# A two-layer graph network on one core: the start of each gather group is granted by SyncE instead of paced by memsets on GpSimd

## The chip, the cores and the metric

The kernel runs on one core of one Trainium2 chip. Its time is the device time of one execution in microseconds (us), taken as the median of three runs. Engines are named as in the profile: PE is TensorE (PEld its weight loads), DVE is VectorE, ACT is ScalarE, POOL is GpSimd, SP is SyncE. A small q behind a name (POOLq, SPq) is the engine's sequencer: register operations, waits, semaphore increments and DMA issues that run there and are not counted as busy time. A semaphore is a counter; an engine waits until it has reached a value, and instructions and DMAs add to it when they end.

## The reference

There are 12500 nodes with 64 features and 212500 edges (source, target, 8 edge features, one of 16 types), sorted by target.

```
h = relu(layernorm(x))
x = x + segment_sum over edges of  h[src] @ W_rel[type],  into dst          # layer 1
h = relu(layernorm(x))
msg = relu(concat(h[src], h[dst], attr) @ W1 + b1) @ W2 + b2
x = x + segment_sum(msg, dst)                                              # layer 2
```

## The kernel before

**Tiling.** The edges are worked through in 208 groups of 1024 (8 tiles of 128 edges), the last one shifted back so that it is full. Eight groups are one turn of a loop (`it` counts 26 turns, `u` the 8 groups of a turn). Layer 1 takes all 208 groups, then layer 2 all 208.

**What a group does.** POOL fetches the 1024 source rows by eight indirect DMAs (`gather`, 128 rows of 256 bytes each): in layer 1 from `h_table`, in layer 2 from `p_table`, which holds h @ W1's upper part. The rows land in `rows[:, u]`, one of eight buffers, and count in `rows_in[u]`. In layer 1 PE multiplies each tile of rows with a one-hot of slot and type that DVE makes (`onehot`) and counts `slots_summed` twice per group; ACT copies the sums (`slots`); every second group PE applies the 16 type weights and places the result (`place`), and DVE adds it to the accumulator `acc`. Once per turn a chunk of 480 finished nodes is normalised and multiplied with W1, and SP stores it to `p_table` and `q_table`. In layer 2 PE makes the edge and target parts of the message (`w_attr`, `q_blk`), DVE adds the gathered rows to them (`slots<-ps,rows`, counted by `pre_added`), ACT applies relu, PE and DVE sum and place.

**What sets the order around the change.** Each engine runs its own program in order; semaphores tie them together. POOL's main loops are `turn_of_rows` (layer 1) and `turn_of_groups` (layer 2). Before group g it waits, in this order, for: `spaced`, that is until all memsets behind the gathers of group g-1 are done; `batch_in`, every fourth group, the indices; `slots_summed` (layer 1) or `pre_added` (layer 2), until the engines have finished group g-2. Then it issues eight pairs of one gather and one memset of a single element, `spacer`, which counts `spaced`. The first 16 groups of layer 1 are outside this: their gathers (six groups from `x`, ten from `h_table` with `src_tab` as index) have no memsets and no wait for `spaced`, and from the seventh on wait only for the group that used the buffer before.

SP's loop in layer 1 (`batch`, `store_pq`) loads the next indices, four groups at a time, when `slots_summed` shows the buffer free, and stores the chunk of the turn before. In layer 2 (`pairs`) it waits every second group for `pre_added`, reads two group bases from SBUF (`TENSOR_LOAD base_row`) and issues two loads of `q_win`; every fourth group it adds a load of indices and one of edge features, once per turn the store of a finished chunk.

`wait_apart` is a wait with an increment of a counter that nobody reads; on the sequencer it is one instruction (`EVENT_SEMAPHORE`), with a register operation ahead of it where the value depends on the loop.

Of the kernel before, what the change touches and what calls it, by code (L numbers as in the profile page):

```python
# [6 lines left out]
def gnn_kernel(nc, x, src, dst, edge_attr, edge_type, rel_weight, w1, b1, w2, b2, out):  # L7
# [23 lines left out]
    T = 8  # L31
# [6 lines left out]
    U = 8  # L38
# [30 lines left out]
    EVEN = (HG - 1) // 16 * 16  # L69
    IDS = 16 * 4  # L70
    assert PG * T == AC * CI and U - EG == PG and EG < U and G % U == 0 and G % 2 == 0 and LN0 + LP * LI == N and 0 < DUP and NC % AC == 1 and U == 8

    ctx = ExitStack()
    with ctx:
# [3 lines left out]
        def sem(name):  # L78
            return ctx.enter_context(nc.semaphore(name))
# [176 lines left out]
        rows_in = [sem(f"rows_in_{u}") for u in range(U)]  # L256
        spaced = sem("spaced")

# [279 lines left out]
        def _(sp):  # L538
# [46 lines left out]
            with sp.If(fits > 0):  # L585
                def batch(it, k):

                    g = it * U + k * B
                    wait_apart(sp, slots_summed, 2 * (g + B))
                    sp.dma_start(idx[:, k * B:(k + 1) * B, :], src_tab[:, bass.ds(g, B), :]).then_inc(batch_in[k], 16)  # L590

                sp.wait_ge(prep_copied, 4)
                sp.wait_ge(weights_in, 16 * NWL)
                sp.dma_start(w_attr[T * F:2 * T * F], w_attr[0:T * F]).then_inc(weights_copied, 16)
                with sp.Fori(2, NIT) as it:
                    for k in range(U // B):
                        batch(it, k)
                    store_pq(it - 2, chunk_nodes)

                for k in range(U // B):  # L600
                    sp.wait_ge(slots_summed, 2 * (AHEAD + G - U + (k + 1) * B))
                    sp.dma_start(idx[:, k * B:(k + 1) * B, :], src_tab[:, k * B:(k + 1) * B, :]).then_inc(batch_in[k], 16)
                store_pq(NC - 1, chunk_nodes)
            with sp.Else():
# [13 lines left out]
            with sp.If(fits > 0):  # L618
# [24 lines left out]

                def pairs(it, ahead=2):

                    for u in range(1, U, 2):
                        g = it * U + u
                        if ahead or u < V:
                            wait_apart(sp, pre_added, AHEAD + g + 1)
                            load_q(g + V - 1, (u + V - 1) % V)  # L650
                        if u % B == B - 1 and (ahead or u < B):
                            k = u // B
                            if ahead:
                                load_idx((it + 1) * U + k * B, k)
                            if ahead == 1 and k == U // B - 1:
                                load_last_attr()
                            else:
                                load_attr((it + 1) * U + k * B if ahead else 0, k)
# [5 lines left out]
                pairs(0)  # L664
                with sp.Fori(1, NIT - 2) as it:
                    pairs(it)
                    store_out(it - 1, chunk_nodes)
                pairs(NIT - 2, ahead=1)
                store_out(NIT - 3, chunk_nodes)
                pairs(NIT - 1, ahead=0)  # L670
                store_out(NC - 1, chunk_nodes)
# [8 lines left out]
        def _(pool):  # L680
# [42 lines left out]
            with pool.If(fits > 0):  # L723
# [28 lines left out]
            with pool.If(fits > 0):  # L752
                def turn_of_groups(it, last=False):
                    for u in range(U):
                        wait_apart(pool, spaced, T * ((NIT - 2 + it) * U + u + 1) - SKIP)
                        if u == 0:
# [4 lines left out]
                        for j in range(SKIP if last and u == U - 1 else 0, T):  # L761
                            gather(p_table, u, j, rows_in[u])
                            pool.memset(spacer[:, j:j + 1], 0.0).then_inc(spaced, 1)  # L763

                with pool.Fori(0, NIT - 1) as it:
                    turn_of_groups(it)
# [772 lines left out]
```

## Time and profile before

| | |
|---|---|
| three runs | 4940.25, 4952.87, 4954.87 us; median 4952.87 |
| profiled execution | 4951.48 us, its span 4949.3 us (2.2 us lie outside the span) |
| POOL busy | 3439.7 us, 69% of the span |
| PE busy | 2744.9 us, 55% |
| DVE, ACT busy | 1470.4 us, 582.2 us |
| chain that ended last | POOL 34%, issue 23%, unknown 21%, PE 12%, DVE 6% |
| gathers in the paced loops | 1533 in layer 1, 1661 in layer 2 |

The span is from the first to the last instruction. A row of the timeline gives the start, the duration, engine, line, operation, what is written and read, a count, and in brackets how long the engine sat idle before it and what ended that; "issue" means that the profile shows nothing that it waited for, "remote" that the semaphore's last change has no instruction that the profile could name.

### The profile page before, as it was taken

The page shows a single profiled execution, that of the slowest core. Times are in us where ns is not written, and L with a number is a line of the kernel's source. Part 1 is how long each engine was busy: PE and PEld are TensorE (multiplying, and loading weights), DVE is VectorE, ACT ScalarE, POOL GpSimd, SP SyncE. Part 2 cuts the span into 40 slices and gives each one's busy share as a digit, 9 for nine tenths or more (in the row PEclk, how much of TensorE's full clock was granted, in tenths as well). Part 3 has the DMA queues.
Part 4 walks back from the last instruction along what each step waited for, and adds up shares of the span by engine and source line. Part 5 has one row for each costly group of instructions (what it writes and reads, how often), then busy time and mean ns, then how long its engine had stood idle before and what let it go on. Part 6 is the DMA issues. An engine that isn't in the chain of part 4 may idle for free.

```text
span 4949.3 us, 40507 instructions
## 1 busy us (share of the span) xinstructions
PE 2744.9 (55%) x10310; PEld 1528.5 (31%) x10310; DVE 1470.4 (30%) x2002; ACT 582.2 (12%) x1139; POOL 3439.7 (69%) x6536
## 2 busy tenths in 40 slices
PE   2656555565565655566655454555555554555555
PEld 1434333343343333333422222222222222222222
DVE  6323222222222222222233332333233232332333
ACT  3111111111111111111110000000000000000000
POOL 7567676676776776676756676777777767767676
PEclk8777777777777767776766666666666666666666
DMA  4111111111111111111111111111111111111111
GB/s 100 21 25 25 27 25 24 24 27 24 25 27 25 25 27 25 24 27 24 25 29 29 29 29 30 29 30 31 29 31 31 29 29 30 29 30 32 28 30 26
DMA packets 391188, 144.16 MB, mean 29 GB/s; under 512 B 321650, under 2 KB 337323, under 8 KB 391163
## 3 DMA queue, kind: packets, MB, share of 16 engines
q0 software_dynamic: 106304, 109.07, 11.5%
q1 hardware_dynamic: 282245, 34.18, 4.8%
q10 hardware_dynamic: 2614, 0.62, 0.1%
q8 instruction: 10, 0.16, 0.0%
q14 instruction: 15, 0.12, 0.0%
HBM read 129.03 MB, written 12.83 MB: 29 GB/s over the span
## 4 chain that ended last, share of the span: by engine, by line
POOL 34%; issue 23%; another core or an unknown queue 21%; PE 12%; DVE 6%; DMA 2%; DVEq 1%; ACT 1%; POOLq 0%; ACTq 0%; SPq 0%
POOL rows L710 31%; PE ps L1462 3%; PE ps L1379 2%; PE ps L1461 2%; POOL spacer L743 2%; PE ps L1466 1%; DVE z_slot L1230 1%; DVE slots L1219 1%; DVE q_blk L1243 1%; DMA rows<-p_table,idx 1%; DVEq L1234 1%; POOL spacer L763 1%; PE ps L1386 1%; DMA rows<-h_table,idx 1%
## 5 line engine op out<-in xcount | busy, mean ns | idle before, releaser
L710 POOL DMA_INDIRECT rows<-p_table,idx x1661 | 1580.3, 951 | 728.9 <-issue 510.2
L710 POOL DMA_INDIRECT rows<-h_table,idx x1533 | 1451.9, 947 | 695.9 <-issue 417.5
L1379 PE MATMUL ps<-onehot,rows 128*64 128x256 f32 x3328 | 742.2, 570 | 500.6 <-DMA rows<-h_table,idx 407.2
L1461 PE MATMUL ps<-w_attr,attr_t 64*128 64x512 f32 x416 | 368.0, 980 | 1087.4 <-DVE q_blk L1243 753.8
L1095 DVE TENSOR_TENSOR onehot<-key,ps 128x2048 f32<-128x2048 f32 x209 | 473.9, 2278 | 532.0 <-remote 344.6
L1379 PEld LDWEIGHTS ps<-onehot,rows 128*64 128x64 f32 x3328 | 364.5, 199 | 787.4 <-issue 693.2
L1219 DVE TENSOR_TENSOR slots<-ps,rows 128x512 f32<-128x512 f32 x208 | 143.8, 692 | 1263.0 <-remote 698.4
L1386 PE MATMUL ps<-w_types,slots 128*128 128x128 f32 x3328 | 464.2, 297 | 86.6 <-issue 85.3
L1386 PEld LDWEIGHTS ps<-w_types,slots 128*128 128x128 f32 x3328 | 430.6, 209 | 163.7 <-issue 157.8
L1461 PEld LDWEIGHTS ps<-w_attr,attr_t 64*128 64x128 f32 x416 | 87.8, 262 | 1125.2 <-issue 1124.8
L1462 PE MATMUL ps<-q_blk,onehot 128*128 128x512 f32 x416 | 405.9, 1077 | 0.0
L890 ACT COPY slots<-ps 128x512 f32<-128x512 f32 x416 | 241.0, 588 | 1020.3 <-remote 456.7
L1466 PE MATMUL ps<-relus,onehot 128*128 128x512 f32 x416 | 336.8, 906 | 0.9 <-DVE z_blk L1226 0.9
L1158 DVE TENSOR_TENSOR acc<-acc,ps 64x128 f32 x208 | 58.2, 280 | 889.7 <-PE ps L1393 519.3
L951 ACT ACTIVATE relus<-slots 128x512 f32<-128x512 f32 x208 | 131.1, 630 | 1421.5 <-DVE slots L1219 1083.4
L1226 DVE TENSOR_TENSOR z_blk<-ps,blocks 128x512 f32<-128x512 f32 x208 | 143.2, 689 | 327.8 <-remote 204.5
L1393 PE MATMUL ps<-place,nodes_t 128*64 128x256 f32 x416 | 150.2, 499 | 130.5 <-ACT nodes_t L894 125.8
L1230 DVE TENSOR_REDUCE z_slot<-z_blk 128x64 f32<-128x512 f32 x208 | 209.2, 1006 | 0.0
L1462 PEld LDWEIGHTS ps<-q_blk,onehot 128*128 128x128 f32 x416 | 96.0, 287 | 271.7 <-issue 271.7
L1243 DVE TENSOR_TENSOR q_blk<-ps,blocks 128x512 f32<-128x512 f32 x208 | 141.4, 680 | 98.7 <-remote 78.7
L1456 PEld LDWEIGHTS ps<-q_win,onehot 128*128 128x128 f32 x416 | 109.4, 266 | 191.5 <-issue 191.5
L1470 PEld LDWEIGHTS ps<-onehot,z_slot 128*65 128x65 f32 x416 | 93.2, 224 | 222.0 <-issue 219.5
(142 smaller groups left out, 1939.3 us busy)
## 6 DMA issues: line engine op xcount, KB each, us to landing
rows<-p_table,idx POOLq DMA_INDIRECT x1661
rows<-h_table,idx POOLq DMA_INDIRECT x1533
attr<-in_edge_attr_dram SPq DMA_DIRECT2D x52, 128.0 KB
q_win<-q_table SPq DMA_DIRECT2D x208, 32.0 KB
p_table<-pq_out SPq DMA_DIRECT2D x25, 120.0 KB
q_table<-pq_out SPq DMA_DIRECT2D x25, 120.0 KB
out_dram<-xs SPq DMA_DIRECT2D x25, 120.0 KB
xs<-in_x_dram SPq DMA_DIRECT2D x6, 480.0 KB, 6.3
```

The lines of the kernel that those rows point to most:

```text
L710: pool.indirect_dma_start(rows[:, u, t, :], None, table, bass.IndirectOffsetOnAxis(ap=at, axis=0)).then_inc(s, 16)
L890: act.copy(to, slot_ps[:, u % 2, t, :].rearrange("p t (r w) -> p t r w", w=W0)).then_inc(slots_copied, 1)
L1095: dve.tensor_tensor(onehot[:, b], key0[:, bass.ds(g, 1), :].rearrange("p a (t c) -> p (a t) c", c=1).broadcast_to([P, T, C0]), iota_ps.rea ...
L1219: dve.tensor_tensor(presum[:, u % 2, 0:T * D], pre_ps[:, u % 2, :], rows[:, u].rearrange("p t d -> p (t d)"), ALU.add).then_inc(pre_added, 1)
L1230: dve.tensor_reduce(z_slot[:, u, 0:D], z_blk[:].rearrange("p (t d) -> p d t", d=D), X, ALU.add).then_inc(z_slotted, 1)
L1243: dve.tensor_tensor(by_tile(q_blk[:, u % 2, :]), q_ps.rearrange("p (a d) -> p a d", a=1).broadcast_to([P, T, D]), own_tile, ALU.mult).then ...
L1379: last = pe.matmul(slot_ps[t % 2 * D:(t % 2 + 1) * D, b, t // 2, :], rows[:, u, t, :], onehot[:, b, t, :], start=True, stop=True)
L1386: last = pe.matmul(nodes_ps, slots[:, b, r, :], w_types[:, r, :], start=(r == 0), stop=(r == R - 1))
L1393: last = pe.matmul(win_ps, nodes_t[:, h * D:(h + 1) * D], place[:, h, :], start=(h == 0), stop=(h == 1))
L1461: pe.matmul(pre_ps[:, u % 2, :], attr_t[half, u // 2, :], w_attr[half].rearrange("k j d -> k (j d)"), start=True, stop=False)
L1462: pe.matmul(pre_ps[:, u % 2, :], oh1_t[:, u, :], q_blk[:, u % 2, :], start=False, stop=True).then_inc(pre_made, 1)
L1466: pe.matmul(z_ps, oh1[:, u, :], relu_rows[:, u % 2, :], start=True, stop=True).then_inc(z_made, 1)
```

## The change

The memsets and the semaphore `spaced` go. Two semaphores come: POOL counts `asked`, SP counts `granted`. At the start of each group POOL waits for its grant, counts `asked` for the next group, waits as before for `batch_in` and for `slots_summed` or `pre_added` of group g-2, and issues the eight gathers one behind the other. SP waits for the request, six times in layer 1 and three times in layer 2 with one increment of the unread counter each, and then counts `granted`. SP's loads and stores are put between the grants: in layer 1 the indices behind the second and sixth grant of a turn and the chunk's store behind the fifth; in layer 2 the `q_win` loads, the indices and the edge features behind every second grant, for the group two before, and the store behind the second.

```
...
+    PACE = (6, 3)
...
-        spacer = sb("spacer", [1, T], fp32)
...
+        def asks(it, u, second):
+
+            return (NIT - 2 if second else -2) * U + it * U + u + (0 if second else 1)
...
+                def turn_of_loads(it, last=False):
+                    for u in range(U):
+                        for _ in range(PACE[0]):
+                            wait_apart(sp, asked, asks(it, u, False))
+                        sp.sem_inc(granted, 1)
+                        if u == 1:
+                            batch(it, 1)
+                        if u == 4:
+                            store_pq(it - 2, chunk_nodes)
+                        if u == 5 and not last:
+                            batch(it + 1, 0)
+                        if u == 5 and last:
+                            first_batch(0)
...
+                def turn_of_pairs(it, ahead=2, first=False, store=True):
+                    for u in range(U):
+                        if not first or u >= 1:
+                            for _ in range(PACE[1]):
+                                wait_apart(sp, asked, asks(it, u, True))
+                            sp.sem_inc(granted, 1)
+                        if u % 2 == 1 and (not first or u >= 3):
+                            before, v = back(it, u, 2)
+                            loads_after(before, v, ahead if u >= 3 else min(ahead + 1, 2))
+                        if u == 1 and store:
+                            store_out(it - 2, chunk_nodes)
...
-                pool.sem_inc(spaced, T)
+                pool.sem_inc(asked, 1)
 
                 def turn_of_rows(it, last=False):
                     for u in range(U):
-                        wait_apart(pool, spaced, T * ((it - 2) * U + u + 1))
+                        wait_apart(pool, granted, asks(it, u, False))
+                        if not last or u < U - 1:
+                            pool.sem_inc(asked, 1)
 
                         if u % B == 0:
                             wait_apart(pool, batch_in[u // B], 16 * (it - 1))
                         wait_apart(pool, slots_summed, 2 * AHEAD + 2 * (it * U + u - 1))
                         for t in range(SKIP if last and u == U - 1 else 0, T):
                             gather(h_table, u, t, rows_in[u])
-                            pool.memset(spacer[:, t:t + 1], 0.0).then_inc(spaced, 1)
...
```

The loop of layer 2 on POOL changes in the same way. `loads_after` is the body of the old `pairs`.

Two places show what stands where. First POOL's program at the start of the layer 1 loop, before. `L710` is the gather, `L359` a wait with a register, a wait that carries no own line stands at the next instruction.

```order
46 L745 UNCONDITIONAL_BRANCH
47 L745 ISA
48 L359 ISA [waits spaced]
49 L359 ISA [waits batch_in_0]
50 L710 DMA rows<-h_table,idx 128x64 [waits slots_summed]
51 L743 MEMSET spacer 1x1
52 L710 DMA rows<-h_table,idx 128x64
53 L743 MEMSET spacer 1x1
```

The same place after the change, with the next group; `L364` is the wait, `L740` the gather.

```order
48 L364 ISA [waits granted]
49 L364 ISA [waits batch_in_0]
50 L740 DMA rows<-h_table,idx 128x64 [waits slots_summed]
51 L740 DMA rows<-h_table,idx 128x64 x7
52 L364 REGISTER_ALU
53 L364 ISA [waits granted]
54 L740 DMA rows<-h_table,idx 128x64 [waits slots_summed]
55 L740 DMA rows<-h_table,idx 128x64 x7
```

A group is now eight gathers in a row, and the wait ahead of it is no longer for work of POOL itself but for a count of SP.

Then SP's loop of layer 1, before: `idx<-src_tab` are the index loads, `p_table` and `q_table` the chunk's stores.

```order
37 L590 ISA [waits slots_summed]
38 L590 DMA idx<-src_tab 128x32
39 L359 ISA
40 L590 ISA [waits slots_summed]
41 L590 DMA idx<-src_tab 128x32
42 L581 ISA [waits pq_copied]
43 L581 DMA p_table<-pq_out 120x256
44 L581 DMA q_table<-pq_out 120x256
```

After the change (the repeated waits and the increments set no row of their own and stand at the next one):

```order
38 L364 REGISTER_ALU [waits asked]
39 L364 ISA [waits asked]
40 L595 ISA [waits slots_summed]
41 L595 DMA idx<-src_tab 128x32
42 L364 REGISTER_ALU
43 L364 REGISTER_ALU [waits asked] x2
44 L586 ISA [waits asked,pq_copied]
45 L586 DMA p_table<-pq_out 120x256
46 L586 DMA q_table<-pq_out 120x256
47 L364 REGISTER_ALU
48 L364 ISA [waits asked]
49 L595 ISA [waits slots_summed]
50 L595 DMA idx<-src_tab 128x32
```

The index loads and the store now stand behind grants, and a grant that follows them in the program waits until they are issued.

## Rows read from the trace of the kernel before

**Rows 1.** The page, part 1: busy time of each engine.

```profile
PE 2744.9 (55%) x10310; PEld 1528.5 (31%) x10310; DVE 1470.4 (30%) x2002; ACT 582.2 (12%) x1139; POOL 3439.7 (69%) x6536
```

**Rows 2.** POOL's groups by line: busy, mean ns | idle before, releasers.

```profile
L710 POOL DMA_INDIRECT rows<-p_table,idx x1661 | 1580.3, 951 | 728.9 <-issue 510.2 <-DVE slots L1219 198.9 <-POOL spacer L763 19.8
L710 POOL DMA_INDIRECT rows<-h_table,idx x1533 | 1451.9, 947 | 695.9 <-issue 417.5 <-remote 193.9 <-PE ps L1379 78.8
```

**Rows 3.** The memsets by tile: ns min/median/max, first and last start.

```profile
L763 POOL MEMSET spacer<- x1661: 88/89/91, 2502.8 to 4926.8; 1x1 f32 x185
L743 POOL MEMSET spacer<- x1533: 88/89/91, 218.3 to 2473.9; 1x1 f32 x192
```

**Rows 4.** Timeline of POOL, layer 1, 1498 to 1584 us.

```profile
1501.17 0.95 POOL L710 DMA_INDIRECT rows<-h_table,idx  x1 [3.63 <-remote]
...
1502.42 0.95 POOL L710 DMA_INDIRECT rows<-h_table,idx  x1 [0.21 <-issue]
...
1511.92 0.95 POOL L710 DMA_INDIRECT rows<-h_table,idx  x1 [0.96 <-issue]
...
1514.00 0.95 POOL L710 DMA_INDIRECT rows<-h_table,idx  x1 [1.04 <-issue]
...
1536.19 0.94 POOL L710 DMA_INDIRECT rows<-h_table,idx  x1 [2.84 <-remote]
...
1581.23 0.95 POOL L710 DMA_INDIRECT rows<-h_table,idx  x1 [1.06 <-issue]
```

**Rows 5.** POOL's waits: total us, times, longest.

```profile
POOL rows L710 <- issue: 971.0, 3161, 27.9
POOL rows L710 <- remote: 205.0, 71, 4.5
POOL rows L710 <- DVE slots L1219: 198.9, 48, 8.4
POOL rows L710 <- PE ps L1379: 83.6, 15, 23.8
```

**Rows 6.** Timeline of POOL, the gathers without memsets, 103 to 194 us.

```profile
103.69 0.94 POOL L710 DMA_INDIRECT rows<-h_table,src_tab  x1 [4.83 <-PE ps L1379]
...
132.44 0.94 POOL L710 DMA_INDIRECT rows<-h_table,src_tab  x1 [0.30 <-issue]
137.89 0.95 POOL L710 DMA_INDIRECT rows<-h_table,src_tab  x1 [4.50 <-remote]
...
160.87 0.94 POOL L710 DMA_INDIRECT rows<-h_table,src_tab  x1 [3.28 <-remote]
...
183.87 0.95 POOL L710 DMA_INDIRECT rows<-h_table,src_tab  x1 [3.30 <-remote]
...
192.63 0.95 POOL L710 DMA_INDIRECT rows<-h_table,src_tab  x1 [0.30 <-issue]
```

**Rows 7.** Timeline of ACT in the same stretch.

```profile
137.47 0.27 ACT L894 COPY nodes_t<-ps 128x128 f32<-128x128 f32 x1 [26.16 <-remote]
...
195.33 0.27 ACT L894 COPY nodes_t<-ps 128x128 f32<-128x128 f32 x1 [6.54 <-remote]
```

**Rows 8.** Timeline of ACT, layer 1, 1520 to 1540 us.

```profile
1535.42 0.59 ACT L890 COPY slots<-ps 128x512 f32<-128x512 f32 x1 [5.09 <-remote]
```

**Rows 9.** Line 745, POOL's loop end, 1523 to 1534 us: ns, starts.

```profile
L745 POOLq ALU_OP  x1: 35/35/35, 1526.8 to 1526.8; - x1
```

**Rows 10.** Sequencer steps by line: ns min/median/max, first and last start.

```profile
L360 POOLq EVENT_SEMAPHORE  x926: 17/17/17, 183.9 to 4920.0; - x186
...
L360 SPq EVENT_SEMAPHORE  x202: 4/17/710, 204.1 to 4946.2; - x101
...
L638 SPq TENSOR_LOAD <-base_row x104: 467/477/737, 2504.9 to 4888.8; - x104
...
L626 SPq FUSED_REGOPS  x46: 5/688/1397, 2651.1 to 4763.2; - x46
```

More of the change, by code:

```diff
@@ L256, in gnn_kernel @@
         rows_in = [sem(f"rows_in_{u}") for u in range(U)]
-        spaced = sem("spaced")
+        asked = sem("asked")
+        granted = sem("granted")
         onehot0 = sem("onehot0")
@@ L594, in _, with first_batch @@
                 sp.dma_start(w_attr[T * F:2 * T * F], w_attr[0:T * F]).then_inc(weights_copied, 16)
[L595 to L600, printed above, removed]
+                def first_batch(k):
                     sp.wait_ge(slots_summed, 2 * (AHEAD + G - U + (k + 1) * B))
                     sp.dma_start(idx[:, k * B:(k + 1) * B, :], src_tab[:, k * B:(k + 1) * B, :]).then_inc(batch_in[k], 16)
+                def turn_of_loads(it, last=False):
[11 more added lines that the diff above has]
+                            first_batch(0)
+                batch(2, 0)
+                with sp.Fori(2, NIT - 1) as it:
+                    turn_of_loads(it)
+                turn_of_loads(NIT - 1, last=True)
+                first_batch(1)
                 store_pq(NC - 1, chunk_nodes)
@@ L642, in load_q, with loads_after @@
                         sp.dma_start(q_win[:, v + b, :], q_table[bass.ds(bases[b], P), :]).then_inc(q_in[v + b], 16)
[L644 to L658, printed above, removed]
+                def loads_after(it, u, ahead=2):
+                    g = it * U + u
+                    if ahead or u < V:
+                        wait_apart(sp, pre_added, AHEAD + g + 1)
+                        load_q(g + V - 1, (u + V - 1) % V)
+                    if u % B == B - 1 and (ahead or u < B):
+                        k = u // B
+                        if ahead:
+                            load_idx((it + 1) * U + k * B, k)
+                        if ahead == 1 and k == U // B - 1:
+                            load_last_attr()
+                        else:
+                            load_attr((it + 1) * U + k * B if ahead else 0, k)
+                def turn_of_pairs(it, ahead=2, first=False, store=True):
[9 more added lines that the diff above has]
+                            store_out(it - 2, chunk_nodes)
                 for k in range(U // B):
@@ L663, in _ @@
                     load_q(v, v)
[L664 to L670, printed above, removed]
+                turn_of_pairs(0, first=True, store=False)
+                turn_of_pairs(1, store=False)
+                with sp.Fori(2, NIT - 2) as it:
+                    turn_of_pairs(it)
+                turn_of_pairs(NIT - 2, ahead=1)
+                turn_of_pairs(NIT - 1, ahead=0)
                 store_out(NC - 1, chunk_nodes)
@@ L752, in _, with turn_of_groups @@
             with pool.If(fits > 0):
-                def turn_of_groups(it, last=False):
+                def turn_of_groups(it, first=False, last=False):
                     for u in range(U):
-                        wait_apart(pool, spaced, T * ((NIT - 2 + it) * U + u + 1) - SKIP)
+                        if not first or u >= 1:
+                            wait_apart(pool, granted, asks(it, u, True))
+                        if not last or u < U - 1:
+                            pool.sem_inc(asked, 1)
                         if u == 0:
@@ L762, in turn_of_groups @@
                             gather(p_table, u, j, rows_in[u])
-                            pool.memset(spacer[:, j:j + 1], 0.0).then_inc(spaced, 1)
-                with pool.Fori(0, NIT - 1) as it:
+                turn_of_groups(0, first=True)
+                with pool.Fori(1, NIT - 1) as it:
                     turn_of_groups(it)
```

## The prediction

> **What bounds the kernel now.** I read the page's busy line first: POOL is at 69% of the span, PE at 55% [rows 1], so no engine is simply full. The groups by line come next: POOL has 3194 gathers of 0.947 to 0.951 us and stands idle ahead of them for 695.9 + 728.9 = 1424.8 us [rows 2]. That idle time is the only thing the change can touch, so I split it with the timeline of POOL, where the number in brackets tells three kinds apart [rows 4].
>
> Within a group a memset of 0.089 us [rows 3] stands between two gathers with 0.21 us of idle behind it, so a gather starts 0.95 + 0.30 = 1.25 us after the one before. At an ordinary group boundary the idle is 0.96 to 1.06 us, with the memset 1.05 to 1.15. And at some boundaries POOL stops: 2.84 and 3.63 us in these rows. The waits give the stops' count: 71 remote, 48 by DVE, 15 by PE, 488.1 us together [rows 5]; less the five or so of the start (the 23.8 and a 4.83 are theirs) about 130 in 399 groups, one after every third group. Stops and boundaries sum up so: idle plus memsets less 0.30 for each gather is 695.9 + 1533 x 0.089 - 1533 x 0.30 = 372 us in layer 1 and 728.9 + 147.8 - 498.3 = 378 us in layer 2; without the start of each layer (23.8 and 27.9) 349 and 350 us. With 191.5 and 207.5 groups that is 1.82 and 1.69 us a boundary. A group is eight gathers, 10.0 us, and so takes 11.8 and 11.7 us; the memsets' own first and last starts say the same: (2473.9 - 218.3) / 191.5 = 11.78 and (4926.8 - 2502.8) / 207.5 = 11.68 [rows 3]. The kernel is bound by this rhythm: ten us of gathers, then on average 1.75 us without.
>
> **What a stop is.** The first gathers of layer 1 show POOL without memsets and without the wait for them. There the gap between two gathers is 0.30 us [rows 6], as now with a memset in it. So the 3194 memsets, 284 us of POOL's busy time, cost nothing by themselves: the gap hides them. And there POOL runs two or three groups on end and then stops for 3.28 to 4.83 us, the releaser "remote". What the other engines do meanwhile is in ACT's row: it has waited 26.16 us when it gets its sums at 137.47, 0.42 us ahead of POOL's restart [rows 7, 6]. PE had been given the rows long before; its counts reached nobody while POOL gathered without a pause, and came some 3 to 4 us after POOL's last gather began. In the loop it is the same in small: ACT waits 5.09 us until 1535.42, and POOL starts at 1536.19 [rows 8, 4]. So an uninterrupted run of gathers holds back the other engines' counts, and a stop is what lets them through. The short pause of 1.05 us at each boundary doesn't by itself do that.
>
> **The change part by part.**
>
> *The memsets.* Removed: 3194 x 0.089. They lie in a gap that stays 0.30 us without them [rows 6]: 0.
>
> *The wait for `spaced`.* It comes when the memsets of the group before are done, so it empties POOL's queue at each boundary: 1.05 us instead of 0.30, 0.75 us too much, at some 270 boundaries that are not stops. It also stalls the program at the loop's end: the sequencer is there at 1526.8, while the third gather of a group still runs [rows 9], so it runs about eleven entries ahead (five gathers, six memsets), and without the wait the next group's gathers would be queued in time. The gap of 1.04 us ahead of the second gather of the seventh group [rows 4], the queue's refill behind such a drain, is then hidden too: 49 turns x (1.13 - 0.30) = 41 us. If POOL's queue doesn't run ahead over the new wait, none of this is gained; that is rival C's ground.
>
> *The new wait on POOL.* `granted` was asked for one group, 10.0 us, before. Queued behind it on POOL are a count, `batch_in`, `slots_summed` or `pre_added` and eight gathers; behind those wait PE, DVE and ACT. POOL's own steps are 17 ns each [rows 10], hidden by the queue. What SP needs: in layer 1 a register operation, six waits, one count, eight steps; in layer 2 five. The trace of before has no such chain. From below: POOL's boundary with a register operation and a wait more takes 1.06 instead of 0.96 us, 0.10 for two steps, so eight take 0.4 us or, at the quickest row, 0.03. From above SP's own rows: a wait up to 0.71 us, a register operation up to 1.40 with a median of 0.69, a load of a base 0.48 to 0.74 [rows 10]. At 0.69 a step the grant comes 5.5 us after the request in layer 1, in time by 4.5; at 1.40 it comes after 11.2, late by 1.2. In layer 2 five steps at 0.69 are 3.4 us; where two window loads precede the grant they add a wait and, twice, a base, an address operation, a move and a DMA, by the same rows some 6 us, 9.4 in all; and where the indices and edge features are added too (two of eight groups), three steps more and a transfer's issue each, about 12.9, late by 2.9. I take the grant as in time, since the value nearest to most rows is the 0.69, and keep the late cases as rival D.
>
> The Trainium skill's page Advanced Engine Details and Errata, section on Network/Comms, says that reading a semaphore from a sequencer takes 50 to 100 ns on trn2; eight steps would by it take an estimated 0.4 to 0.8 us, the grant would be nine us early, and the sum would stay as it is below. [...]
>
> *SP's loads and stores* keep the conditions they had; POOL waits for the same group's `slots_summed` or `pre_added` as SP, so a load put between grants isn't late by that. The cover of this is the one group of lead; where it is gone, it is D's price.
>
> *What is late next.* With the drains gone, POOL runs on until `slots_summed` or `pre_added` of group g-2 is not there, which by the early stretch is after two or three groups. Start to start, without memsets: 137.89 - 103.69 = 34.20 us for three groups; 160.87 - 137.89 = 22.98 and 183.87 - 160.87 = 23.00 for two [rows 6]. The restart behind ACT's was 0.42 us there, in the loops 0.77 [rows 7, 8, 6, 4], so I add 0.35: 34.55 / 3 = 11.52 and 23.35 / 2 = 11.67 us a group. At the kernel's present third I weigh three-group runs twice: (2 x 11.52 + 11.67) / 3 = 11.57.
>
> **The sum.** 399 groups x 11.57 = 4616.4 us, against 2473.9 - 218.3 + 4926.8 - 2502.8 = 4679.6 now: 63.2 us saved. The profiled execution took 4951.48 (its span and 2.2 us more), 1.4 below the median of 4952.87. 4951.5 - 63.2 = 4888, taken as 4890. Its own range: a group at 11.42 to 11.67 gives 4557 to 4656, that is 4830 to 4930.
>
> **The rivals.**
>
> *B, the boundaries shrink and the stops stay as they are.* If the stops come by the group's own work and not by the length of POOL's run, then 270 x 0.75 = 202 us go and nothing replaces them: 4951.5 - 202 = 4749, with the 41 us of refills 4708. For it: the stops number only 130 and many groups start on time. Against it: the early rows, where 0.30 boundaries bring stops every two or three groups of up to 4.83 us. Chance 0.17, centre 4750.
>
> *C, nothing moves.* The other engines may need a fixed time free of gathers for each group, whatever its form; then the 0.75 us that the boundaries lose, the stops gain. For it: 1.82 and 1.69 us a boundary now are not far from (34.20 - 30.0) / 3 = 1.40 and (22.98 - 20.0) / 2 = 1.49 in the early stretch, and that stretch has no chunk to normalise and no store, so it may need less. Against: it is less by 0.2 to 0.4 us a group. That the change does nothing of what it says, POOL's queue stopping at the register wait as long as now, ends here too. 4940 to 4965; chance 0.16.
>
> *D, the grant becomes the stop.* While POOL gathers without a pause, SP steps slowly, and now SP's steps stand in POOL's path. It decides where a layer 1 grant needs more than 10.0 / 8 = 1.25 us a step, in layer 2 on the two loaded groups of a turn. Late by 1.2 us at 192 groups of layer 1 is 230 us, by 2.9 at 26 x 2 groups of layer 2 is 151, together 381; SP's waits have their median at 0.017 and its address operations at 0.688, so I take the steps as held half of the time, 190 on top of the forecast: 4888 + 190 = about 5080. The bound: a stop after every single group; after a run of one group POOL would restart 10.0 us of gathers, 195.33 - 193.58 = 1.76 us after the last gather's end (192.63 + 0.95) and 0.77 behind that, 12.5 us a group [rows 6, 7], 399 x 12.5 = 4988, 308 more than now, 5260. For it: SP's steps of 0.69 to 1.40 us [rows 10]. Against: a late grant is itself a pause, and in a pause SP's steps are short, so it ends itself. Chance 0.26.
>
> **How the numbers follow.** Forecast A 0.41, B 0.17, C 0.16, D 0.26. The three runs lie 14.6 us apart, 0.3%, which is what can be told from no change. Faster are A, nearly all, and B: 0.57, with 0.01 of A's upper end counted as no change; no change is C with that end, 0.17; slower is D, 0.26. The range leaves out the upper third of D and the lower edge of B: 4710 to 5100; the forecast's own is 4830 to 4930.
>
> **What would show it.** Right: gathers at 1.25 us in a group and over most boundaries, idle 0.30 there; stops of 3.5 to 5 us after two or three groups, released by a count of PE, ACT or DVE; 11.5 to 11.7 us a group in both layers; the 1.04 us gap gone where no stop is near. B shows 130 stops or fewer at unchanged length. D shows stops whose releaser is SP's count, and SP's waits at 0.7 us or more ahead of them. Wrong I would be if most boundaries are still 1 us (the queue doesn't run over the grant), if the gap without memsets is not 0.30, or if the runs of groups are much shorter than two or longer than three.

## The result, and the profile after

The changed kernel takes 5065.2 us in the median of four runs (5036.68 to 5109.91), the kernel before 4952.51 beside it: 1.0241 of it, with an interval of 1.016 to 1.0321. Faster was forecast; it is slower, though by how much is less sure: measured again beside other runs of both (e14), the changed kernel was at 1.0071. The profiled execution is the quickest of the four, 5036.68 us with a span of 5034.5.

Busy times of the changed kernel, in the columns of [rows 1]:

```profile
PE 2739.4 (54%) x10310; PEld 1521.2 (30%) x10310; DVE 1470.7 (29%) x2002; ACT 577.8 (11%) x1139; POOL 3166.0 (63%) x3342
```

POOL's gathers by line (busy, mean ns | idle before, releasers), against [rows 2]:

```profile
L740 POOL DMA_INDIRECT rows<-p_table,idx x1661 | 1581.7, 952 | 871.4 <-issue 499.6 <-DVE slots L1253 321.6 <-DMA p_table<-pq_out 26.0
L740 POOL DMA_INDIRECT rows<-h_table,idx x1533 | 1450.8, 946 | 914.4 <-issue 438.1 <-PE ps L1413 274.7 <-remote 201.2
```

POOL's waits (total us, times, longest), against [rows 5]:

```profile
POOL rows L740 <- issue: 981.0, 3112, 6.1
POOL rows L740 <- DVE slots L1253: 321.6, 61, 11.3
POOL rows L740 <- PE ps L1413: 279.6, 54, 23.8
POOL rows L740 <- remote: 220.4, 85, 5.4
...
POOL rows L740 <- SPq L684: 16.2, 7, 4.2
POOL rows L740 <- SPq L608: 0.3, 1, 0.3
```

Without the memsets POOL is busy for 274 us less and the gathers are as long as before, but the idle time has grown by more than that: the waits for PE's, DVE's and other counts went from 487.5 (205.0 + 198.9 + 83.6; the prediction's 488.1 was a slip) to 821.6 us. From the timeline of both I took for each group the time from the last gather's end to the next one's start, memset included, and count over 2 us as a stop:

| | before | after |
|---|---|---|
| layer 1: ordinary boundaries, mean | 112 of 1.08 us | 92 of 0.43 us (78 of them 0.3) |
| layer 1: stops, sum, mean | 79, 254 us, 3.22 | 99, 435 us, 4.39 |
| layer 1: per group | 11.77 us | 12.21 us |
| layer 2: ordinary boundaries, mean | 160 of 1.11 us | 144 of 0.35 us (139 of 0.3) |
| layer 2: stops, sum, mean | 47, 203 us, 4.31 | 63, 343 us, 5.44 |
| layer 2: per group | 11.68 us | 11.69 us |

The ordinary boundaries lose 81 + 127 = 208 us, as the change's part of the sum had it (202). The stops gain 181 + 140 = 321. With some 25 us of refill gaps gone that is 88 us more, against 85.2 by the two spans. Of the 208 us some 40 are 36 boundaries that turned into stops; the others became shorter by 0.65 and 0.76 us. And the whole loss lies in layer 1: in layer 2 the stops took back what the boundaries gave, and a group takes 11.69 us as before.

TensorE's clock isn't the cause: the granted clock is 0.690 of full speed in the mean before and 0.684 after, PE is busy for no more time (2739.4 us against 2744.9), e1 below is faster than before at 0.681 to 0.688, and the one run of e7 with a recorded clock of 1.0 was the slowest of its ten (4971 us).

One run of two groups shows how. POOL's timeline after the change:

```profile
1526.47 0.95 POOL L740 DMA_INDIRECT rows<-h_table,idx  x1 [3.37 <-PE ps L1413]
...
1536.48 0.95 POOL L740 DMA_INDIRECT rows<-h_table,idx  x1 [0.31 <-issue]
...
1545.24 0.94 POOL L740 DMA_INDIRECT rows<-h_table,idx  x1 [0.30 <-issue]
1550.04 0.95 POOL L740 DMA_INDIRECT rows<-h_table,idx  x1 [3.85 <-remote]
```

PE and then ACT in the same time:

```profile
1537.83 3.35 PE L1413 MATMUL ps<-onehot,rows 128*64 128x256 f32 x16 [3.20 <-DMA rows<-h_table,idx]
1549.43 1.54 PE L1427 MATMUL ps<-place,nodes_t 128*64 128x256 f32 x3 [8.25 <-ACT nodes_t L928]
```

```profile
1530.91 0.59 ACT L924 COPY slots<-ps 128x512 f32<-128x512 f32 x1 [0.75 <-PE ps L1413]
1549.11 0.27 ACT L928 COPY nodes_t<-ps 128x128 f32<-128x128 f32 x1 [17.61 <-remote]
```

PE ends a group's 16 products at 1541.2. ACT, which only has to be told of such sums, starts nothing between 1531.5 and 1549.11, the whole second group and 2.9 us beyond its last gather (1545.24 + 0.94), and PE idles 8.25 us for ACT. The trace's semaphore records have the times of the counts themselves, and they are what is late: the product that ACT waits for here ends at 1534.6 (the last of the type weights), its count stands at 1549.09; the products that end at 1539.8 and 1541.2 are counted at 1549.18 and 1549.27. The windows put the two groups and the stop in numbers; columns are the stretch, its length, busy us of each engine and its instructions, TensorE's granted clock, DMA share and GB/s. After the change:

```profile
1502.70:1513.40 10.70, 10.05 (x33) 5.54 (x34) 3.57 (x4) 2.26 (x5) 7.57 (x9) 0.51 0.13 26
1513.40:1523.10 9.70, 6.12 (x39) 4.00 (x38) 1.63 (x1) 0.00 (x0) 7.56 (x8) 0.85 0.22 49
...
1526.50:1536.50 10.00, 8.12 (x52) 6.01 (x50) 5.55 (x5) 1.45 (x3) 7.56 (x9) 0.81 0.12 23
1536.50:1546.20 9.70, 3.35 (x16) 1.95 (x16) 0.00 (x0) 0.00 (x0) 7.55 (x8) 0.71 0.14 27
```

Before, the first group behind a stop, a second behind a boundary of 1.04 us (and 1.13 us more behind its first gather, the refill gap of [rows 4]), and a third behind a boundary of 1.04 us:

```profile
1501.20:1511.90 10.70, 7.87 (x52) 5.88 (x50) 5.55 (x5) 1.45 (x3) 8.24 (x16) 0.82 0.15 26
1511.90:1522.60 10.70, 5.99 (x24) 3.16 (x24) 1.27 (x3) 2.32 (x5) 8.31 (x16) 0.55 0.12 21
1522.60:1533.30 10.70, 7.56 (x45) 5.74 (x45) 3.68 (x5) 0.59 (x1) 8.22 (x16) 0.84 0.12 25
```

Behind a boundary ACT works 2.32 us on five instructions and then 0.59 on one before; after the change, in both second groups, 0.00 on none. So the rest of about 1 us that I had counted as pure loss was the time in which the others' counts came through. The group of 1511.90 had the refill gap beside its rest, so here is a count over all of layer 1 that leaves such groups out: what ACT starts in the first 10 us of a group, for second groups (behind an ordinary boundary, the group before being behind a stop) and third groups (behind two ordinary boundaries).

| | groups | ACT starts, mean | groups with none | end in a stop |
|---|---|---|---|---|
| before, second | 45 | 2.04 | 0 | 21 |
| before, third | 41 | 0.54 | 23 | 38 |
| after, second | 86 | 0.58 | 51 | 81 |

So one rest buys one more group in layer 1, and not a third: there ACT starts as little as after the change, although a rest of 1.09 us stands ahead of it.

The longest stops of layer 1, twelve of 8.3 to 9.1 us and all ahead of the eighth group of a turn, are the same thing with more behind it. In one of them the hold ends at 1473.07, 2.9 us after the last gather, but by then the chunk's copy and two groups' sums have piled up:

```profile
1469.20 0.94 POOL L740 DMA_INDIRECT rows<-h_table,idx  x1 [0.30 <-issue]
1479.13 0.94 POOL L740 DMA_INDIRECT rows<-h_table,idx  x1 [8.99 <-PE ps L1413]
```

```profile
1473.07 0.27 ACT L928 COPY nodes_t<-ps 128x128 f32<-128x128 f32 x1 [17.91 <-remote]
1473.31 0.59 ACT L877 COPY stage<-acc 64x480 f32 x1
1476.68 0.59 ACT L924 COPY slots<-ps 128x512 f32<-128x512 f32 x1 [2.78 <-PE ps L1413]
1478.38 0.59 ACT L924 COPY slots<-ps 128x512 f32<-128x512 f32 x1 [1.12 <-PE ps L1413]
```

The grant was not what POOL waited for in layer 1. SP's step that counts `granted` for the group of 1550.04, ahead of which POOL stops, stands at 1530.6 (line, steps, ns, starts):

```profile
L608 SPq EVENT_SEMAPHORE  x1: 16/16/16, 1530.6 to 1530.6; - x1
```

By the records of POOL's sequencer, all 99 stops of layer 1 end with `slots_summed`; the grant was there 8 us or more before the restart. In layer 2 `granted` was still missing at 32 of the 63 stops when POOL's last gather ended, but at all except 9 of these `pre_added` came later still. The 9, which end with the grant, last 31 us together, so a late grant alone can't be the loss; what grants and SP's new order do besides, the experiments had to tell.

### The profile page after: what moved, and what is told of

The parts are those of the page before. It is cut to its first block, busy times and chain, and to the rows that moved or that the text cites. A ratio compares the mean times of both kernels' runs of the same rounds, so it can differ in the third digit from the quotient of the medians.

```text
span 5034.5 us, 40195 instructions
## 1 busy us (share of the span) xinstructions
PE 2739.4 (54%) x10310; PEld 1521.2 (30%) x10310; DVE 1470.7 (29%) x2002; ACT 577.8 (11%) x1139; POOL 3166.0 (63%) x3342
## 4 chain that ended last, share of the span: by engine, by line
another core or an unknown queue 36%; PE 24%; issue 22%; DVE 8%; POOL 6%; DVEq 1%; DMA 1%; ACT 1%; SPq 0%; POOLq 0%; ACTq 0%
PE ps L1413 7%; POOL rows L740 6%; PE ps L1496 4%; PE ps L1495 4%; PE ps L1500 2%; PE ps L1427 2%; DVE q_blk L1277 2%; PE ps L1420 1%; DVE z_slot L1264 1%; DVE slots L1253 1%; PE ps L1378 1%; PE ps L1380 1%; DVEq L1268 1%; DVE z_blk L1260 1%
## 5 line engine op out<-in xcount | busy, mean ns | idle before, releaser
L740 POOL DMA_INDIRECT rows<-p_table,idx x1661 | 1581.7, 952 | 871.4 <-issue 499.6
L740 POOL DMA_INDIRECT rows<-h_table,idx x1533 | 1450.8, 946 | 914.4 <-issue 438.1
L1413 PE MATMUL ps<-onehot,rows 128*64 128x256 f32 x3328 | 728.4, 557 | 438.3 <-DMA rows<-h_table,idx 297.3
L1420 PE MATMUL ps<-w_types,slots 128*128 128x128 f32 x3328 | 445.5, 291 | 64.7 <-issue 63.9
L1420 PEld LDWEIGHTS ps<-w_types,slots 128*128 128x128 f32 x3328 | 413.3, 203 | 131.0 <-issue 118.9
L1427 PE MATMUL ps<-place,nodes_t 128*64 128x256 f32 x416 | 167.1, 544 | 255.8 <-ACT nodes_t L928 208.4
L1427 PEld LDWEIGHTS ps<-place,nodes_t 128*64 128x64 f32 x416 | 75.7, 195 | 339.6 <-ACT nodes_t L928 235.4
```

The source lines that it names most:

```text
L740: pool.indirect_dma_start(rows[:, u, t, :], None, table, bass.IndirectOffsetOnAxis(ap=at, axis=0)).then_inc(s, 16)
L1413: last = pe.matmul(slot_ps[t % 2 * D:(t % 2 + 1) * D, b, t // 2, :], rows[:, u, t, :], onehot[:, b, t, :], start=True, stop=True)
L1420: last = pe.matmul(nodes_ps, slots[:, b, r, :], w_types[:, r, :], start=(r == 0), stop=(r == R - 1))
L1427: last = pe.matmul(win_ps, nodes_t[:, h * D:(h + 1) * D], place[:, h, :], start=(h == 0), stop=(h == 1))
```

## The experiments

Theories: **P**, the missing rest of about 1 us at the boundaries costs the time. **G**, the grant comes late. **M**, the memsets between the gathers are what lets the counts through. The kernel before was measured again beside every set of experiments, and ratios are to it; it took 4951 to 4952 us beside e1 to e7 and 5004 to 5010 beside e8 to e16. "Boundary" is the time without a gather at ordinary boundaries (memset included), stops are over 2 us, both from each kernel's one profile, layer 1 / layer 2.

| kernel | ratio, interval | boundary us | stops, mean us | us a group |
|---|---|---|---|---|
| changed | 1.0241, 1.016 to 1.0321 | 0.43 / 0.35 | 99, 4.39 / 63, 5.44 | 12.21 / 11.69 |
| e1 changed + one rest | 0.9942, 0.9924 to 0.9961 | 1.33 / 1.32 | 72, 3.07 / 27, 4.21 | 11.76 / 11.52 |
| e2 neither rest, memsets nor grants | 1.0356, 1.0278 to 1.0435 | 0.47 / 0.43 | 93, 4.30 / 62, 7.41 | 12.05 / 12.26 |
| e4 changed, one wait per grant | 1.0182, 1.0137 to 1.0228 | 0.33 / 0.34 | 95, 4.46 / 59, 6.05 | 12.09 / 11.73 |
| e3b memsets, no rest | 1.0089, 1.0071 to 1.0106 | 0.37 / 0.38 | 111, 3.39 / 72, 3.95 | 11.86 / 11.73 |
| e6 rest of 1.0 by work | 1.0058, 1.0038 to 1.0078 | 1.00 / 0.99 | 79, 3.91 / 49, 4.66 | 11.90 / 11.63 |
| e7 one memset, rest by drain | 0.9982, 0.9958 to 1.0007 | 1.10 / 1.09 | 73, 3.28 / 36, 5.23 | 11.72 / 11.63 |
| e5 two rests a group | 0.9879, 0.9862 to 0.9895 | 1.09 / 1.10 | 27, 2.49 / 0 | 11.62 / 11.55 |
| e8 changed + two rests | 0.9911, 0.9883 to 0.9939 | 1.33 / 1.34 | 17, 2.31 / 0 | 11.78 / 11.77 |
| e9 two rests of 0.62 | 0.9959, 0.9937 to 0.9982 | 0.65 / 0.62 | 93, 3.32 / 50, 5.60 | 11.94 / 11.90 |
| e10 one rest of 0.61 | 1.0212, 1.0156 to 1.0268 | 0.67 / 0.67 | 95, 4.73 / 56, 6.90 | 12.36 / 12.08 |
| e11 a rest every 6 gathers | 0.9889, 0.9863 to 0.9916 | at 11 of 64 gathers | 68, 2.89 / 30, 4.67 | 11.83 / 11.69 |

In the count of ACT's starts from above, second groups have 1.75 in e1, 1.96 in e7 and 1.78 in e6, all with a rest of 1 us and more, 1.12 in e10, 1.03 in e3b and 1.09 in e2. e9's profile is of its slowest run (5029 us, median 4987), so its stops may count too high.

**e1: give the changed kernel its rest back.** One memset behind a group's last gather, and a wait for it; the grants stay (layer 1 shown, layer 2 alike).

```
+                        wait_apart(pool, spaced, (it - 2) * U + u + 1)
                         wait_apart(pool, granted, asks(it, u, False))
...
                             gather(h_table, u, t, rows_in[u])
+                        pool.memset(spacer[:, 0:1], 0.0).then_inc(spaced, 1)
```

> The changed kernel, grants and all, with one memset behind each group's last gather and POOL's wait for it at the next boundary: the boundary's rest of about 1 us is back, seven of eight memsets are not. Theory P (the rest of 1 us at each boundary is what lets the other engines' counts through; without it the second group of a run stays held): ordinary boundaries at 1.0 us again, 11.7 to 11.8 us a group in layer 1, no stops of 6 to 9 us, 4930 to 4980. Theory G (the time is lost because the grant comes late): the grant is as late as before, 5040 to 5110. Theory M (a memset between two gathers is what lets the counts through): as the changed kernel, 5040 to 5110, with 7 of 8 memsets missing.

Measured 4918.9 us, below the whole range of P and out of reach of G and M: 146 us under the changed kernel, and faster than before. The boundary is 1.33 us, since the grant's steps now stand behind the drain:

```profile
1510.68 0.09 POOL L779 MEMSET spacer<- 1x1 f32 x1
1511.96 0.94 POOL L742 DMA_INDIRECT rows<-h_table,idx  x1 [1.19 <-issue]
```

**e2: no rest, no memsets, no grant.** SP's program as before.

```
-                        wait_apart(pool, spaced, T * ((it - 2) * U + u + 1))
...
-                            pool.memset(spacer[:, t:t + 1], 0.0).then_inc(spaced, 1)
```

> The kernel before without memsets, without the wait for them, and without any grant; SP's loops as before. Theory P: the boundaries have 0.30 us and the stops grow as in the changed kernel: 12.1 to 12.3 us a group in layer 1, 5030 to 5110. Theory G: with no grant to wait for the forecast of 4890 comes true, 4830 to 4930. Theory M: 5030 to 5110.

Measured 5138 us. G fails: with no grant to wait for it is no faster. P holds in direction, but 5138 lies above P's range and above the changed kernel: in layer 2 a group takes 12.26 us here and 11.69 there.

**e4: shorter chain ahead of the grant.**

```
-    PACE = (6, 3)
+    PACE = (1, 1)
```

> The changed kernel with one wait instead of six (layer 1) and three (layer 2) ahead of each grant: SP's chain is 3 steps long. Theory P: the grant isn't what is waited for in layer 1, and in layer 2 pre_added takes its place: 5030 to 5110. Theory G: the grant comes 2 to 7 us earlier where steps are slow, and the time falls towards 4890, at least below 4990. Theory M: 5030 to 5110.

Measured 5036 us. In layer 2 the grant is now missing when POOL runs dry at 8 of 59 stops (32 of 63 before this edit) and is the last count at 4 (9), but the stops' sum is 357 us against 343: nothing is won there. The time is within P's range, and the interval overlaps the changed kernel's.

**e3b: memsets without the rest.** The wait is for memsets eight groups back.

```
-                pool.sem_inc(spaced, T)
+                pool.sem_inc(spaced, U * T)
...
```

> The kernel before with all eight memsets a group; POOL's wait at the boundary is for memsets eight groups back, which are long done, so there is no rest at the boundary and no grant. Theory P (the rest of about 1 us at each boundary lets the other engines' counts through): stops as without memsets, 5050 to 5150. Theory M (a memset between two gathers does it): no worse than before, 4880 to 4960.

Measured 4990 us, outside both expectations: slower than before, which fits P, but far below e2's 5138, so the memsets do something that P doesn't name. There are more stops than in e2, but shorter ones (3.4 and 4.0 us). Nor is it quite without rests: 16 gaps inside groups of layer 1 and 67 of layer 2 are over 0.6 us long (109 us together), against 4 and 2 in e2. Whether these make the difference is not settled.

**e6: a rest by work.** POOL's queue never drains; a memset of 128x840 takes the rest's place.

```
...
-                            pool.memset(spacer[:, t:t + 1], 0.0).then_inc(spaced, 1)
+                        pool.memset(spacer[:, u % 2, :], 0.0).then_inc(spaced, 1)
...
```

> The kernel before without its eight memsets; behind each group's last gather stands one memset of 128x840 elements (by the 128x492 one of the start, 0.511 us, about 0.87 us long), and POOL's wait is for the one two groups back: POOL has a rest of 1.0 to 1.2 us between groups, but its queue never drains. Theory P1 (it is enough that POOL's engine doesn't gather for 1 us): 4900 to 4970, ordinary boundaries at about 0.3 us idle beside the memset, no stops above 6 us in layer 1. Theory P2 (POOL's queue has to run empty): stops as without a rest and the memset's time on top, 5080 to 5300.

```profile
1520.64 0.82 POOL L743 MEMSET spacer<- 128x840 f32 x1
1521.63 0.95 POOL L710 DMA_INDIRECT rows<-h_table,idx  x1 [0.17 <-POOL spacer L743]
```

Measured 4973 us, 3 us above P1's range and far from P2's: 0.99 us without a gather brings most of it, and the queue need not run empty. Two signs go against P1 in full: layer 1 still has stops of up to 9.0 us, which it excluded, and e7, whose queue drains, is 0.8% faster, with intervals apart.

**e7: one memset, the drain, no grant.**

```
...
-                            pool.memset(spacer[:, t:t + 1], 0.0).then_inc(spaced, 1)
+                        pool.memset(spacer[:, 0:1], 0.0).then_inc(spaced, 1)
...
```

> The kernel before with one memset a group, behind the last gather, in place of eight, and the wait for it at the boundary; no grant. Theory P: the boundary's rest is there, so 4900 to 4960. If the first experiment's gain over the kernel before came from the seven memsets less, it is here too: 4905 to 4930; if it came from the grants, 4940 to 4960.

Measured 4935 us (4922 to 4971), between the two sub-cases; whether e1's further gain comes from the grants or from its longer rest isn't told apart.

**e5: two rests a group.**

```
...
+                            if t % 4 == 3:
+                                pool.memset(spacer[:, 0:1], 0.0).then_inc(spaced, 1)
+                            if t == 3:
+                                wait_apart(pool, spaced, 2 * ((it - 2) * U + u) + 3)
```

> As the one before, with a second memset and a second wait behind the fourth gather of each group: a rest of about 1 us every 5 us. Theory P, with the held state setting in 6 to 8 us after a rest (in the kernel before ACT's rate falls from 0.27 to 0.08 starts per us there): the held state doesn't come, hardly any stops, 10.0 + 2 x 0.75 = 11.5 us a group, 4951 - 399 x (11.73 - 11.5) = about 4860, 4830 to 4900. If the other engines need their time whatever the rests: no faster than with one rest, 4910 or above.

Measured 4887.9 us, all four runs within 1.7 us: P's range. Its waits show hardly any stop left:

```profile
POOL rows L710 <- issue: 1377.7, 3113, 26.8
POOL rows L710 <- remote: 84.3, 38, 4.6
POOL rows L710 <- POOL spacer L767: 76.2, 88, 1.0
POOL rows L710 <- POOL spacer L744: 72.1, 80, 1.0
```

Layer 2 has no stop at a boundary and 11.55 us a group, which is eight gathers and two rests: POOL's own program is the bound there.

**e8: two rests in the changed kernel.** The edit of e5 in the changed kernel.

> The changed kernel, grants and all, with one memset and POOL's wait for it behind the fourth and behind the eighth gather of each group. Theory P (what costs the time is the missing rest): two rests a group, as in the kernel with two rests and no grants, 4850 to 4910, no stops in layer 2. Theory G (late grants cost the time): stops that end with the grant stay, 4950 or above.

Measured 0.9911, no stop in layer 2: P by its sign. By the time alone, 4964 us, it would be G's: P's range misses by 54 us, and the kernel before took 5010 here, 58 more than when the range was set. Beside e5 the grant's steps only lengthen the rest by 0.24 us a group.

**e9 and e10: shorter rests by work.** A memset of 128x400 behind the fourth and eighth gather (e9), behind the eighth alone (e10).

> The kernel before, with a memset of 128x400 elements (about 0.4 us by the 0.82 us of 128x840) behind the fourth and the eighth gather of each group and no wait that drains POOL's queue: two rests of 0.55 to 0.65 us a group in place of 1.0. If so short a rest is enough to let the counts through, and the other engines aren't the bound: 10.0 + 2 x 0.3 = 10.6 us a group and up to 11.2 with a few stops, 4951 - 399 x (11.73 - 10.6 to 11.2) = 4500 to 4740. If it isn't enough: stops as without a rest, 4970 to 5150. If it is enough and the other engines are the bound at some 11.5 us a group: 4850 to 4900.

> As the kernel with one memset of 128x840 behind each group (4973 us, a rest of 1.0 us), with 128x400 in its place: a rest of 0.55 to 0.65 us. If the rest's length doesn't matter as long as there is one: 399 x 0.4 = 160 less where no stop follows, 4840 to 4960. If it has to last about 1 us: the stops of 6 to 9 us in layer 1 are back, 4990 to 5150.

```profile
1499.36 0.45 POOL L743 MEMSET spacer<- 128x400 f32 x1
1499.97 0.95 POOL L710 DMA_INDIRECT rows<-h_table,idx  x1 [0.17 <-POOL spacer L743]
...
1508.72 0.94 POOL L710 DMA_INDIRECT rows<-h_table,idx  x1 [0.31 <-issue]
1509.67 0.45 POOL L743 MEMSET spacer<- 128x400 f32 x1
1513.40 0.95 POOL L710 DMA_INDIRECT rows<-h_table,idx  x1 [3.29 <-remote]
```

```profile
1499.90:1510.10 10.20, 3.68 (x16) 1.92 (x16) 0.00 (x0) 0.00 (x0) 7.99 (x9) 0.50 0.14 26
```

The length matters. In e10 the group behind a rest of 0.61 us (1499.97; the second fence has the windows' columns) has DVE and ACT at 0.00, as behind 0.30, and the kernel is at 1.0212, the second case of its expectation. Two such rests (e9) bring 0.9959, with about as many stops as e10 but shorter ones: 4987 us lies in the range of its second case, the ratio (4931 of 4951) under it.

**e11: a rest every six gathers.**

```
+                            if (T * u + t + 1) % 6 == 0 or T * u + t + 1 == U * T:
+                                pool.memset(spacer[:, 0:1], 0.0).then_inc(spaced, 1)
+                                wait_apart(pool, spaced, 11 * (it - 2) + -(-(T * u + t + 1) // 6))
```

> The kernel before without its eight memsets; one memset and POOL's wait for it behind every sixth gather of a turn (11 rests in 64 gathers, in place of 16 in the kernel with two rests a group, 0.988 of before). Theory P, with the held state not yet harmful at 7.5 us after a rest: 10.0 + 11 / 8 x 0.75 = 11.0 to 11.2 us a group, 399 x (11.73 - 11.0 to 11.2) = 210 to 290 us less, 0.94 to 0.96 of the kernel before. If the held state sets in within 7.5 us and a rest of 1.05 us then comes too late: stops of 3 us and more are back, 11.5 or above, 0.98 to 1.00. If the other engines are the bound at 11.5: 0.98 to 0.99 too, with short stops.

Measured 0.9889, the middle case: stops of 2.9 and 4.7 us are back. Five us between rests keep layer 2 free of stops, 7.5 do not; what the shorter total of rests gives, the stops take, and the time is e5's within the intervals. Whether the longer runs or the fewer rests bring the stops back isn't told apart.

**e12 to e16: what the grant itself does.** e12 and e16, the same kernel twice, take POOL's wait for the grant out of layer 2, e13 out of both layers; SP's program stays the changed one. e14 is the changed kernel, e15 is e2, and e13 to e16 were measured side by side on one chip. The first two lines are layer 2's, the last is layer 1's.

```
-                        if not first or u >= 1:
-                            wait_apart(pool, granted, asks(it, u, True))
...
-                        wait_apart(pool, granted, asks(it, u, False))
```

> The changed kernel, but in layer 2 POOL doesn't wait for the grant; SP's program is unchanged, so its loads stand where the change put them. In layer 2 the changed kernel took 11.69 us a group, the one with neither rests nor grants 12.26. If the wait for the grant is what helps there (it breaks a run of gathers): 12.2 us a group again, 1.035 to 1.05 of the kernel before. If it is the new place of SP's loads: 11.7, 1.015 to 1.03. Theory G (late grants cost time): faster than the changed kernel, below 1.015.

> The changed kernel, but POOL never waits for a grant; SP counts grants that nobody waits for, and its loads stand where the change put them. If POOL's wait for the grant gives time (it breaks runs of gathers): slower than the changed kernel, as the kernel with neither, 1.03 to 1.045. If SP's new order of loads gives it: as the changed kernel, 1.015 to 1.03. If the grant costs time (theory G): faster than the changed kernel, 1.00 to 1.015.

> The changed kernel itself, on the same chip as the other three: 1.016 to 1.032 of the kernel before by its own runs; layer 1 at 12.0 to 12.25 us a group and layer 2 at 11.65 to 11.75 if one profile speaks for the others.

> The kernel with neither rests nor grants and SP's old order, on the same chip: 1.028 to 1.044 by its own runs. If grants and SP's order matter to nothing, the same as the changed kernel here.

> The changed kernel without POOL's wait for the grant in layer 2, on the same chip: 1.006 to 1.011 by its own runs. If the wait in layer 2 costs time: 1 to 2 per cent below the changed kernel again. If it gives time: above it, with layer 2 at 11.9 us a group or more and layer 1 as there.

| | ratio, interval | median us |
|---|---|---|
| e12: no wait in layer 2 (measured with e11) | 1.0085, 1.0057 to 1.0113 | 5047.8 |
| e15: neither, SP's old order | 1.0245, 1.021 to 1.0281 | 5132.3 |
| e13: SP's new order, POOL waits for no grant | 1.013, 1.0087 to 1.0173 | 5080.3 |
| e16: the wait in layer 1 alone | 1.0108, 1.0083 to 1.0133 | 5054.2 |
| e14: changed | 1.0071, 1.0046 to 1.0096 | 5035.8 |

By itself e12 spoke for G, 1.6% below the changed kernel's first ratio, and e13 lies in the band named for G as well. Side by side that falls, since there the changed kernel is lower than e13 and no higher than e16: the wait in layer 2 makes no loss (e16 against e14, intervals that overlap), both waits together bring 44 us by the medians (e13 to e14, intervals that just overlap) and SP's new order 52 (e15 to e13, intervals apart). e14 came out at 1.0071, below its own earlier interval, and e15 at 1.0245, below the range named for it: the kernel before is 51 us slower here than beside the first result, the changed one 29 us faster. The sign is the same in both, the size is not. The chip is not the reason, e1, e2 and e4 ran on the same one with before at 4951; the granted clocks moved along (before from 0.69 to 0.68, changed from 0.68 to 0.70), which may be cause or effect. Why the times moved stays open.

## Why the prediction was wrong

**The memsets, 0.** The gap within a group is 0.30 us without them, as forecast. That they cost nothing to remove is not borne out: e3b, with memsets and no rest, is at 1.0089 where e2, with neither, is at 1.0356 (1.0245 when measured again). So this step failed too, beside the one below: with the rest gone the memsets were worth 1.6 to 2.7%, more than the 0.9% that the rest's going costs while they stay. With the rest in place seven of eight are worth nothing (e7).

**The wait for `spaced`.** POOL's queue does run on over the boundary, 0.30 us at 217 of 236 ordinary ones, and gaps over 0.6 us inside a group fell from 49 to 20. The 202 us of that term were measured as 208, in part by luck, as the 36 boundaries that became stops are in it.

**The step that failed** is the sentence under "What a stop is": "The short pause of 1.05 us at each boundary doesn't by itself do that", meaning let the held counts through. It does. I had read it from the stops alone: since a stop of 3 us was needed now and then, I took the short pauses to be useless. The trace of before already spoke against it, in a row I hadn't looked for: ACT works 2.32 us in a group behind such a boundary, and starts 2.04 instructions in ten us of a second group where after the change it starts 0.58. e1, e6 and e7 put the rest back in three ways and the time came back with it; e10, with 0.61 us, did not. The sentence holds for third groups alone (0.54).

**The stops.** By the sum they were to grow by 202 - 63 = 139 us, or by 180 with the 41 us of refill gaps; they grew by 321. Layer 2 came out at the 11.5 to 11.7 us a group that was forecast, layer 1 at 12.21. The early stretch [rows 6] from which I took 11.4 to 11.5 us a group had no chunk to normalise behind the hold; in the loop the stops last 4.39 and 5.44 us in the mean, and up to 9 and 11 us. (The counts' "3 to 4 us after POOL's last gather began" are 5.0 and 2.7 by [rows 6] and [rows 7].)

**The new wait.** In time in layer 1, as taken. In layer 2 the grant is often late, but the last count at only 9 of 63 stops. The prices were off: by the sequencers' records a grant comes 2.2 us after its request in the median of layer 1 (5.5 was taken) and 9.1 in layer 2, but over 10 us after it at 39 of 192 and 94 of 207. It is also not so that SP's waits are slow only while POOL gathers: they take 17 ns in the median in runs of gathers (gaps under 0.6 us) and outside them, in both kernels, and after the change over 0.1 us at 382 of 1675 in runs and at 54 of 300 outside.

**The rivals.** D named 5080 and 5065 came, by luck, for its mechanism isn't the cause: a late grant would have made the kernels without a wait for it faster than the changed one beside them, and e13 and e15 are slower. B fails, since stops became more and longer. C describes layer 2, where boundaries lost 127 us and stops gained 140; it fails in layer 1, 81 against 181, and the time free of gathers isn't fixed: e5 needs 1.6 us a group, the changed kernel 2.2 in layer 1. The range held the time for a reason that wasn't in it.

## What to carry to other kernels

When one engine's stream holds up the others, a short pause in it that looks like loss may be what keeps them going: before counting it as a gain, look at what the waiting engines do in the stretch right behind such a pause, not only in the long stops. Then place pauses by the length of run that the others stand: here a rest of 1 us every 5 us of gathers beat both kernels, 0.988 of the kernel before, without any handshake. And compare a stretch with another only if the same work is due in both.

## What the runs showed of the hardware

While POOL gathers with gaps of 0.30 us, the counts of other engines arrive late: PE's of 1534.6 stood at 1549.09, 2.9 us after the run's last gather. A rest of POOL of 0.99 to 1.1 us lets them through for one more group of 10 us (2.04 starts of ACT in layer 1's second groups, 0.54 in third ones), one of 0.61 us hardly (e6, e10: 1.0058 and 1.0212); it need not drain POOL's queue. Rests every 5 us leave no stop at layer 2's boundaries (e5), rests every 7.5 us leave 30 (e11). Memsets of 0.09 us between gathers, in a gap that is mostly 0.30 us either way, are worth time where there is no rest (e3b against e2), for a reason that no run shows. What inside the chip holds the counts, no run shows either.
